# Where the row statistics and one of four sine products are computed in the first stage of a transformer layer on one core

## What is computed

```python
def _layernorm(x, axis=-1, eps=1e-05):
    m = jnp.mean(x, axis=axis, keepdims=True)
    v = jnp.var(x, axis=axis, keepdims=True)
    return (x - m) / jnp.sqrt(v + eps)
...
    Q = jnp.einsum('bsd,ed->bse', x, Wq).reshape(b, s, NUM_HEADS, D_K).transpose(0, 2, 1, 3)
    K = jnp.einsum('bsd,ed->bse', x, Wk).reshape(b, s, NUM_HEADS, D_K).transpose(0, 2, 1, 3)
    V = jnp.einsum('bsd,ed->bse', x, Wv).reshape(b, s, NUM_HEADS, D_K).transpose(0, 2, 1, 3)
    Q = _rope(Q)   # even*cos - odd*sin, even*sin + odd*cos
    K = _rope(K)
...
x = x + _L0_attn_ref(_layernorm(x, axis=-1), L0_attn_Wq, L0_attn_Wk, L0_attn_Wv, L0_attn_Wo)
x = x + _L0_ffn_ref(_layernorm(x, axis=-1), L0_ffn_w1, L0_ffn_b1, L0_ffn_w2, L0_ffn_b2)
```

## Time and profile before

| | us |
|---|---|
| median of 3 runs | 2092.21 |
| lowest, highest | 2088.59, 2093.59 |
| the profiled execution's own time | 2093.28 |
| its span (first to last instruction) | 2091.5 |
| first matmul of stage 2 | 227.89 |

### The profile page before, as it was taken

How to read it: one execution, slowest core, us unless ns; L and a number is a source line. 1 busy time by engine, 2 the same in 40 slices (tenths; PEclk the granted TensorE clock), 3 DMA queues, 4 the chain that set the end, 5 groups by cost and what they waited for, 6 DMA issues and landing times. The chain is left out here.

```text
span 2091.5 us, 53450 instructions
## 1 busy us (share of the span) xinstructions
PE 1944.1 (93%) x19104; PEld 781.3 (37%) x19104; DVE 1874.4 (90%) x4039; ACT 1473.9 (70%) x3092; POOL 636.9 (30%) x1265
## 2 busy tenths in 40 slices
PE   5787499999999999999999999999999879999998
PEld 3444022222222222222232222222222246777776
DVE  7999799999999999999999999999999157777775
ACT  5665078888888888888888888888888823323232
POOL 7999522121222212222122221222212323333331
PEclk9999589999999999999999999999999989999999
DMA  5666530321303213042230322304210212222220
GB/s 174 225 207 216 162 62 23 79 42 44 69 23 79 41 45 69 23 79 40 47 69 23 79 37 49 69 23 79 40 37 19 72 57 86 86 86 81 82 83 26
DMA packets 133319, 153.17 MB, mean 73 GB/s; under 512 B 23904, under 2 KB 99424, under 8 KB 132832
## 3 DMA queue, kind: packets, MB, share of 16 engines
q1 hardware_dynamic: 133088, 150.19, 27.6%
HBM read 90.38 MB, written 59.77 MB: 72 GB/s over the span
## 5 line engine op out<-in xcount | busy, mean ns | idle before, releaser
L879 ACT ACTIVATE s_prob<-s_ps 128x512 f32<-128x512 f32 (+3 forms) x2560 | 1198.3, 537 | 177.3 <-PE s_ps L722 145.1
L807 DVE TENSOR_REDUCE s_part<-s_ps 128x2 f32<-128x1024 f32 x768 | 875.1, 1219 | 7.4 <-PE s_ps L705 7.1
L741 PE MATMUL s_ps<-s_prob,s_v 128*32 128x256 f32 (+3 forms) x10240 | 736.6, 359 | 14.8 <-ACT s_o L870 12.1
L705 PE MATMUL s_ps<-mk,mq 64*128 64x512 f16 (+3 forms) x2560 | 680.6, 356 | 52.4 <-DVE s_part L807 21.2
L722 PE MATMUL s_ps<-aq,ak 64*128 64x512 f16 (+3 forms) x2560 | 714.1, 351 | 5.2 <-ACT s_prob L879 2.3
L909 POOL TENSOR_SCALAR_AFFINE_SELECT s_prob<-s_prob 128x128 f32<-128x128 f32 x1024 | 286.5, 292 | 1089.0 <-ACT s_prob L879 1071.4
L814 DVE CUSTOM_DVE_ANT_0 s_ps<-s_ps,mask_sb 128x512 f32<-128x512 f32 (+3 forms) x1024 | 463.3, 538 | 2.8 <-PE s_ps L705 1.9
L741 PEld LDWEIGHTS s_ps<-s_prob,s_v 128*32 128x32 f32 x10240 | 201.9, 108 | 433.9 <-issue 213.5
L722 PEld LDWEIGHTS s_ps<-aq,ak 64*128 64x128 f16 x2560 | 176.1, 93 | 489.6 <-ACT s_prob L879 459.1
L705 PEld LDWEIGHTS s_ps<-mk,mq 64*128 64x128 f16 x2560 | 166.2, 93 | 124.1 <-DVE s_part L807 50.7
L1177 ACT ACTIVATE s_h_f<-s_ps,s_b_s 128x512 f32<-128x512 f32 x128 | 87.9, 687 | 107.4 <-PE s_ps L1042 86.4
(11 more groups left out here) (88 smaller groups left out, 1581.3 us busy)
## 6 DMA issues: line engine op xcount, KB each, us to landing
v_scratch<-s_vst SPq DMA_DIRECT2D x32, 512.0 KB, 4.0
s_v<-v_scratch SPq DMA_DIRECT2D x16, 1024.0 KB, 11.6
att_scratch<-s_o SPq DMA_DIRECT2D x64, 256.0 KB, 2.4
aq<-qk_scratch SPq DMA_DIRECT2D x96, 128.0 KB, 4.4
ak<-qk_scratch SPq DMA_DIRECT2D x96, 128.0 KB, 7.0
s_xin<-x SPq DMA_DIRECT2D x16, 512.0 KB, 4.4
qk_scratch<-s_r_lo SPq DMA_DIRECT2D x64, 128.0 KB, 2.2
qk_scratch<-s_r_hi SPq DMA_DIRECT2D x64, 128.0 KB, 2.3
```

Of the source, the lines that this page charges most:

```text
L705: nc.tensor.matmul(ps[:, bank_of(use + jj), 0:w], mq[rows, p, pair, qt * P:(qt + 1) * P], mk[rows, p, pair, kc * CH:kc * CH + w], start=Tr ...
L741: last = nc.tensor.matmul(ps[32 * j:32 * j + 32, O_BANK, cols], v[:, p, kb, j, :], prob[:, s % 2, j, cols], start=kb == 0 and part == 0, s ...
L807: nc.vector.tensor_reduce(part[:, qt // TPC, :, pair, qt % TPC, kc], ps[:, bank_of(use):bank_of(use) + 2, 0:w], AX.X, ALU.max).then_inc(m_ ...
L879: nc.scalar.activation(prob[:, s % 2, j, q0:CH], ps[:, s_bank(s, j), q0:CH], ACT.Exp, scale=1.0 / (SQK * DK ** 0.5)).then_inc(p_done, 1)
```

## The change

The statistics move, and one of the four products with sin does.

- Chunks 0 and 1 keep VectorE's statistics. From chunk 2 on ScalarE adds up the rows: `totals` reads x with an accumulator output (its main output goes to xn and is overwritten later), VectorE makes the negated mean of it (`mean_of`), ScalarE squares x - mean with an accumulator (`squares_of`) and takes the root.
- VectorE makes 1/std and, new, shift = -mean/std, now behind rope 3. ScalarE's `normalize` is one instruction a block (x * rstd + shift) where x - mean and the product with 1/std were two.
- Of group 3 VectorE multiplies PSUM with sin before the shuffle (sin_part), the shuffle reads that from SBUF, and GpSimd only subtracts (the sign in sin belongs to the row before the shuffle).

```diff
+            def mean_of(n, p):
+                dve.wait_ge(total_done, n + 1)
+                nc.vector.tensor_scalar(negmean[:, p, :], total[:, p, :], -1.0 / D, None, ALU.mult).then_inc(mean_done, 1)
...
                 nc.vector.reciprocal(rstd[:, p, :], std[:, p, :]).then_inc(rstd_done, 1)
+                dve.wait_ge(rstd_done, n + 1)
+                nc.vector.tensor_tensor(shift[:, p, :], negmean[:, p, :], rstd[:, p, :], ALU.mult).then_inc(shift_done, 1)
...
-                nc.vector.stream_shuffle(rot_b[:, g], ps[:, QK_BANK + g], [r ^ 1 for r in range(32)]
-                                         ).then_inc(rot_read, 1)
+                if g == SIN_FIRST:
+
+                    nc.vector.tensor_tensor(sin_part[:], ps[:, QK_BANK + g], sin[:, tok], ALU.mult).then_inc(sin_part_done, 1)
+                    dve.wait_ge(sin_part_done, n + 1)
+                    dve.sem_inc(shuffling, 1)
+                nc.vector.stream_shuffle(rot_b[:, g], sin_part[:] if g == SIN_FIRST else ps[:, QK_BANK + g],
+                                         [r ^ 1 for r in range(32)]).then_inc(rot_read, 1)
...
+                        if g == SIN_FIRST:
+
+                            nc.gpsimd.tensor_tensor(rot_a[:, g], rot_a[:, g], rot_b[:, g], ALU.subtract).then_inc(rot_done, 1)
+                            continue
...
+            def totals(n, p, use):
+                act.wait_ge(x_in[p], 16 * (use + 1))
                 if not isinstance(n, int) or n > 1:
                     act.wait_ge(xt_ready, n - 1)
                 for t in range(TPC):
-                    last = nc.scalar.activation(xn[:, p, t, :], xin[:, p, t, :], ACT.Identity, bias=negmean[:, p, t:t + 1])
-                last.then_inc(centred, 1)
...
+                    last = nc.scalar.activation(xn[:, p, t, :], xin[:, p, t, :], ACT.Identity,
+                                                accum_out=total[:, p, t:t + 1])
+                last.then_inc(total_done, 1)
+
+            def squares_of(n, p):
+                act.wait_ge(mean_done, n + 1)
                 for t in range(TPC):
-                    last = nc.scalar.activation(xn[:, p, t, :], xn[:, p, t, :], ACT.Copy, scale=rstd[:, p, t:t + 1])
+                    last = nc.scalar.activation(xn[:, p, t, :], xin[:, p, t, :], ACT.Square,
+                                                bias=negmean[:, p, t:t + 1], accum_out=squares[:, p, t:t + 1])
+                last.then_inc(squares_done, 1)
+                act.wait_ge(squares_done, n + 1)
+                nc.scalar.activation(std[:, p, :], squares[:, p, :], ACT.Sqrt, bias=eps[:], scale=1.0 / (D * SX ** 2)
+                                     ).then_inc(std_done, 1)
+
+            def normalize(n, p):
+                act.wait_ge(shift_done, n + 1)
+                for t in range(TPC):
+                    last = nc.scalar.activation(xn[:, p, t, :], xin[:, p, t, :], ACT.Identity, bias=shift[:, p, t:t + 1],
+                                                scale=rstd[:, p, t:t + 1])
                 last.then_inc(xn_done, 1)
```

More of the change, by code:

```diff
@@ L206, in stage1 @@
         mv = sb("s1_mv", [P, 2, TPC, 2], F32)
+        total = sb("s1_total", [P, 2, TPC], F32)
         negmean = sb("s1_negmean", [P, 2, TPC], F32)
+        squares = sb("s1_squares", [P, 2, TPC], F32)
+        shift = sb("s1_shift", [P, 2, TPC], F32)
         std = sb("s1_std", [P, 2, TPC], F32)
@@ L213, in stage1 @@
         rot_b = sb("s1_rot_b", [P, NG, CH], F32)
+        sin_part = sb("s1_sin_part", [P, CH], F32)
         r_hi = sb("s1_r_hi", [P, NG, CH], F16)
@@ L238, in stage1 @@
         MANY = NC + 1
+        SIN_FIRST = NG - 1
         def steps(step, engine):
@@ L355, in _, with first_mean_of @@
         def _(dve):
-            def statistics(n, p, use):
-                dve.wait_ge(x_in[p], 16 * (use + 1))
+            def first_mean_of(n, p):
+                dve.wait_ge(x_in[p], 16)
                 for t in range(TPC):
                     nc.vector.bn_stats(stats[:, p, t, :], xin[:, p, t, :]).then_inc(stats_done, 1)
-            def aggregate(n, p):
                 dve.wait_ge(stats_done, TPC * (n + 1))
@@ L397, in step @@
                 rope(n, cc, 1)
+                if left > 2:
+                    mean_of(n + 2, p)
                 if not first:
                     split_rot(n - 1, 3)
-                if left > 2:
-                    statistics(n + 2, p, 2 * b + cc // 2 + 1)
-                    aggregate(n + 2, p)
                 rope(n, cc, 2)
-                if left > 2:
-                    invert_std(n + 2, p)
                 if left > 1:
@@ L408, in step @@
                 rope(n, cc, 3)
+                if left > 2:
+                    invert_std(n + 2, p)
                 split_rot(n, 0)
@@ L415, in _ @@
             for n in range(2):
-                statistics(n, n, 0)
-                aggregate(n, n)
+                first_mean_of(n, n)
                 if n == 1:
@@ L451, in _, with first_std_of @@
         def _(act):
-            def std_of(n, p):
+            def first_std_of(n, p):
                 act.wait_ge(mv_done, n + 1)
@@ L493, in step @@
                     hi_rot(n - 1, 2)
+                    if left > 2:
+                        totals(n + 2, p, 2 * b + cc // 2 + 1)
                     stage_v(n - 1, 0)
@@ L496, in step @@
                     stage_v(n - 1, 1)
+                elif left > 2:
+                    totals(n + 2, p, 2 * b + cc // 2 + 1)
                 if left > 1:
@@ L499, in step @@
                 if left > 2:
-                    std_of(n + 2, p)
-                    centre(n + 2, p)
+                    squares_of(n + 2, p)
                 hi_rot(n, 0)
+                hi_rot(n, 1)
                 if left > 2:
-                    scale_rows(n + 2, p)
-                hi_rot(n, 1)
+                    normalize(n + 2, p)
             act.sem_inc(v_copied, 2)
+            act.sem_inc(total_done, 2)
+            act.sem_inc(squares_done, 2)
             act.wait_ge(eps_preset, 1)
             for n in range(2):
-                std_of(n, n)
-                centre(n, n)
-                scale_rows(n, n)
+                first_std_of(n, n)
+                normalize(n, n)
                 if n == 0:
```

15 lines of the change are left out of this document (6 added, 9 removed).

## The result

| | before | after |
|---|---|---|
| median | 2092.65 (6 runs, 2088.59 to 2093.89) | 2078.88 (6 runs, 2077.81 to 2080.50) |
| span of the profiled execution | 2091.5 | 2076.6 |
| first matmul of stage 2 | 227.89 | 213.01 |
| one chunk (start to start) | 12.23 | 10.98 |

The changed kernel takes 0.9938 of the time before (95% interval 0.9928 to 0.9947): 13.8 us faster, where the prediction said 2093 with a range of 2083 to 2103. All of it lies in stage 1: its end comes 14.88 earlier, and what follows takes as long as before (2076.6 - 213.01 = 1863.6, 2091.5 - 227.89 = 1863.6; over the profiled executions of all kernels run here this untouched part takes 1862.0 to 1868.0).

What follows compares the result with a forecast made beforehand. VectorE and GpSimd taking turns at an exclusive lock bound stage 1, at 12.27 a chunk against 12.23. Periods +0.5, chunk 0 -1.2, before it +0.2, end +1.2: together +0.7, forecast 2093, range 2083 to 2103.

Steps and rivals of the forecast that it cites:

- The step that failed: VectorE, group 0: r_lo(n-1, 3) waits from about 1.3 for GpSimd's sum (1.41 to 2.68) and takes 2.56 to 3.09.
- the timetable: One stage 1 chunk laid out for VectorE and GpSimd from instruction prices: new period 12.27 against 12.23.
- the subtraction: GpSimd, group 3: it and r_lo(n, 0) ask within 0.03; period 12.27 if r_lo goes first, 12.37 if the subtraction does.
- by the number of inputs in SBUF: VectorE against GpSimd: two SBUF inputs mean waiting for the lock; instructions with at most one do not wait.
- the waits stay as they are: Faster rival, stage 1: VectorE's 11.24 becomes the period, -11.9, about 2081; chance 0.22, of which 0.08 for half of it.
- Twelve periods: Stage 1, from rope of chunk 1 to that of chunk 13: +0.04 x 12 = +0.5.
- The start and chunk 0: Shift ahead of xt_lo before chunk 0, +0.2; GpSimd's idle 1.35 in chunk 0 goes, -1.2.
- The end: End of stage 1: r_lo(12, 3) ends 4.9 after rope(13, 0) starts, where it was 3.7, so +1.2.
- ScalarE's accumulator read: Eight reads a chunk on ScalarE, taken at 0.15 each between 0.03 and 0.30; ScalarE's additions hidden, 0.
- A gap is missed: Slower rival: accumulator read over 0.33, so the negated mean waits for sum 0; +0.8 a chunk, about 2103; chance 0.14.
- The clock: Slower rival on TensorE: new gaps lower its clock; +4 a chunk, 2140, if a whole chunk ran at half rate; chance 0.03.

Runs made afterwards that it cites:

- delay3_ahead: Changed kernel with three tiny unused VectorE reciprocals added between the negated mean and r_lo(n-1, 3): 2095.73, chunk 12.22.
- delay1_ahead: Changed kernel with one tiny unused VectorE reciprocal added between the negated mean and r_lo(n-1, 3): 2095.68, chunk 12.22.
- delay3_pin: Changed kernel with three tiny reciprocals ahead of r_lo(n-1, 3), and GpSimd's sum of group 0 made to wait for that r_lo's end: 2085.96, chunk 11.39.
- stats_only: Changed kernel with group 3's sine product put back on GpSimd, so only the statistics move: 2090.67, chunk 12.06.
- mean_behind: Changed kernel with the negated mean placed behind r_lo(n-1, 3) and not ahead of it: 2095.90, chunk 12.25.
- sin13: Changed kernel with the sine product of group 1 on VectorE as well as that of group 3: 2108.07, chunk 13.03.
- best1_delay3: Changed kernel's instructions in another order on VectorE and ScalarE, plus three tiny reciprocals ahead of r_lo(n-1, 3): 2114.39, chunk 13.52.
- pin: Changed kernel with GpSimd's sum of group 0 made to wait for the end of r_lo(n-1, 3): 2085.50, chunk 11.20.

## Why the prediction was wrong

**The step that failed** is the first one of the timetable: "r_lo(n-1, 3) has waited for it since about 1.3, takes 2.56 to 3.09". In the trace it does not wait. The timetable let the negated mean slip in before the sum, and the sum start at 1.41 before r_lo asked. In fact negated mean and r_lo follow each other in 0.06 (103.41 and 103.47) and both are through before GpSimd's sum gets hold of the port. The estimate of r_lo's time, "about 1.3", even lay ahead of the sum's 1.41; I read the two as a tie and gave it to GpSimd without looking at the other outcome. At the subtraction, where the two also asked within 0.03, the text does work out both outcomes (12.27 and 12.37). At the sum of group 0 the other outcome was worth 1.25 a chunk, 15 us, and had no place among the rivals. The three runs with the r_lo delayed or the order enforced (delay3_ahead, delay1_ahead, delay3_pin) show that it is this step: with the sum first, the rest of the timetable holds to 0.05 us (12.22 for 12.27), and with r_lo forced to go first the gain is back. That the tie fell to r_lo was luck of the change's timing; nothing in its code sees to it.

**What of the mechanism held.** The port is taken in turns, tiny instructions included; the shift waits until GpSimd lets go (0.26 from start to start in the kernel after, up to 1.1 in stats_only); r_lo's pair keeps its wait (2.35 for two, 2.55 in the earlier trace rows). Stages 2 and 3 stayed as they were. What the prediction said of who waits, by the number of inputs in SBUF, does not cover the negated mean: it has one, and waits like shift with two (1.24 and 1.18 in stats_only). The reciprocals of the same size and with one input do not (0.17 at 97.78 in delay1_ahead, beside the sum of 97.78). No run here isolates what parts the two.

**The rival that came nearest** is "the waits stay as they are", 11.24 a chunk and 2081. Its number was nearly right, its reason only partly: the wait of the negated mean (0.34) went, the pair's shrank by 0.2, and the shift brought a new one of 0.2, which makes 10.9; 10.98 was measured. The halves run alone, 2090.67 and 2103.76, show that waits do not in general stay as they are.

**Term by term.**
- Twelve periods: +0.5 forecast, 12 x (10.98 - 12.23) = -15.0 measured. This is the whole error.
- The start and chunk 0: +0.2 and -1.2 forecast. Rope of chunk 1 starts at 34.45 after 35.27, -0.8: chunk 0 took 1.29 less (11.46 for 12.75) and began 0.47 later. That beginning lies anywhere from 22.04 to 23.34 in the kernels run here. Sizes right.
- The end: +1.2 forecast from the rope of chunk 13 to SyncE's first load for stage 2, since r_lo(12, 3) would wait there too. It did not, and the stretch took 5.80 (166.25 to 172.05) after 5.74 (182.01 to 187.75): +0.1. From that load to the first matmul the forecast had no change; there are 213.01 - 172.05 = 40.96 us, before 40.14: +0.8. So the sum is near, for a reason that was not the forecast's.
- ScalarE's accumulator read, taken at 0.15 between 0.03 and 0.30, costs 0.09 to 0.10 from start to start. The squares take 0.40 + 0.09 each, as taken; the plain sums only 0.31 + 0.09, where 0.40 + 0.15 was taken. Timeline of ScalarE after:

```profile
98.18 2.07 ACT L497 ACTIVATE s_xn<-s_xin,s_shift,s_rstd 128x256 f32<-128x256 f32 x4 [0.64 <-DVE s_shift L383]
...
100.67 0.42 ACT L480 ACTIVATE s_xn<-s_xin 128x256 f32<-128x256 f32 x1
101.00 0.19 ACT L480 ACTIVATION_READ_ACCUMULATOR s_xn<-s_xin 128x1 f32 x1
101.09 0.40 ACT L480 ACTIVATE s_xn<-s_xin 128x256 f32<-128x256 f32 x1
...
105.21 0.50 ACT L487 ACTIVATE s_xn<-s_xin,s_negmean 128x256 f32<-128x256 f32 x1
105.61 0.19 ACT L487 ACTIVATION_READ_ACCUMULATOR s_xn<-s_xin,s_negmean 128x1 f32 x1
105.70 0.50 ACT L487 ACTIVATE s_xn<-s_xin,s_negmean 128x256 f32<-128x256 f32 x1
```

- What the prediction had missed: normalize, now with two operands from memory, takes 1.98 for four from start to start (98.18 to the next instruction at 100.16) against 1.60 before, 24% more. In all ScalarE has some 10.0 of its own in a chunk, 10.5 was forecast, and it waits 0.30 and 0.64 a chunk. It hides, as said, but with 0.9 to spare it is no longer far from the bound.
- "A gap is missed" needed reads of over 0.33; they cost a third of that, so the rival had no ground. But stats_only, mean_behind and sin13 are that mechanism at work, from other causes, for 1.1 at each gap missed.
- The clock: the new gap of TensorE is there (1.82 for the transposes) and harmless as forecast. The gap of 3.38 of the earlier trace rows is gone, and with it the matmuls at the lower rate: the granted clock is 1.00 in all full chunks, where before it was 0.82 to 0.90 in about every second. The clock is not where the gain comes from: before, those chunks lasted as long as the ones near 1.00, all 12.21 to 12.27.

The Trainium skill (SBUF — State Buffer, Who interferes with whom) says, of VectorE in a two-port mode, that whoever issues first gets the shared pair for the whole instruction, and in general that issue order decides who blocks. The rows agree on the order: r_lo at the same hundredth as the sum held it up (1.82), r_lo 0.09 later was held up by it (1.73). They do not bear out the whole instruction for r_lo: it held the sum for 1.82 - 1.27 = 0.55, and its own row lasts 0.69. I had cited the section for the lock and had not asked it who goes first.

**Open.** What decides a tie. At 0.01 us the starts of the rows do not tell it: in the changed kernel r_lo wins also where its row starts 0.01 behind the sum's, in sin13 and best1_delay3 shift loses at 0.01 behind GpSimd's subtraction (97.92 and 97.91 above). R_lo there has a user of the port directly ahead of it, shift a reciprocal, which is none; whether that matters no run isolates. No run moves one engine by less than 0.09.

## What to carry to other kernels

Where two engines share something exclusive, a timetable from rows is a tree and not a line: at each place where both ask within about 0.1 us, follow both branches to the end of the period, and give each a chance and a price. Here one branch was worth 15 us and the prices were good to 0.03. Moving a little work in front of such a place can cost more than ten times its own length (0.09 us cost 1.24 a chunk here), so a change should be judged with the whole order around it, and halves of a change say little about the whole.

## What the runs showed of the hardware that was not expected

- The port changes hands sooner than a semaphore allows. GpSimd stopped at the port for r_lo was done 1.82 after r_lo's start; made to wait for its semaphore, 2.04. Of the 0.22, 0.14 is the rest of r_lo's row, which lasts on for that long after the port is free (0.69 against 0.55), and 0.08 passes from the row's end to the start of the sum (106.17 to 106.25 in pin). So pinning this order with a wait cost 0.22 us a chunk, more than the lead that it protects.
- An instruction of 4 elements a row waits for the port as long as one of 512: 1.24 (negated mean) and 1.18 (shift) in stats_only, each worth 0.06 to 0.08 when free.
- ScalarE's read of an accumulator is a row of 0.19 us but costs 0.09 to 0.10; an activation over 128x256 costs 0.31 from start to start without an operand from memory, 0.40 with one, 0.50 with two.
